# A graph-attention kernel in which ScalarE writes the exponentials twice, once to PSUM and once to SBUF

## The reference, cut to what matters

```
Qh = (h @ WQ).reshape(N, H, D);  Kh = (h @ WK).reshape(N, H, D);  Vh = (h @ WV).reshape(N, H, D)
Eh = (edge_attr @ WE).reshape(-1, H, D)
score = einsum('ehd,ehd,ehd->eh', Kh[src], Qh[dst], Eh) * inv_sqrt_d
score = exp(clip(score, -5.0, 5.0))
msg = Vh[src] * score[:, :, None]
wV = segment_sum(msg, dst, num_segments=N)
Z = segment_sum(score, dst, num_segments=N)
x = _layernorm(x + (wV / (Z[:, :, None] + 1e-06)).reshape(N, H * D))
```

## Time and profile before

| | us |
|---|---|
| median of three runs | 2854.36 |
| the three runs | 2850.20, 2854.36, 2856.99 |
| the profiled execution | 2860.5 |
| its span, first to last instruction | 2858.7 |

### The profile page before, as it was taken

The page is one execution under the profiler, slowest core; times in us unless marked ns, Lnnn a source line. Parts: engine busy times, 40 slices in busy tenths (PEclk is TensorE's granted clock), DMA queues, the critical chain, the costliest instruction groups (busy, mean ns, idle before and its releaser), DMA issues.

```text
span 2858.7 us, 39244 instructions
## 1 busy us (share of the span) xinstructions
PE 1845.5 (65%) x10440; PEld 1536.1 (54%) x10441; DVE 1490.2 (52%) x3796; ACT 1373.7 (48%) x3309; POOL 1581.0 (55%) x1629
## 2 busy tenths in 40 slices
PE   6266766767667666566666667566656676666676
PEld 5255655555555555455555555455555565555565
DVE  4154455555555555555554555555555555555567
ACT  3144554444544544454444444444444454444455
POOL 7435565555555555555555555555555565555540
PEclk9677677676777777777777777877777777777678
DMA  8335444444444444444444444444444444444431
GB/s 244 104 114 166 126 131 121 124 121 126 126 124 124 125 126 120 122 126 124 121 125 119 120 122 125 127 119 126 124 121 124 118 131 124 122 126 124 122 114 38
DMA packets 281405, 356.25 MB, mean 125 GB/s; under 512 B 144640, under 2 KB 177615, under 8 KB 281186
## 3 DMA queue, kind: packets, MB, share of 16 engines
q0 software_dynamic: 76864, 209.29, 24.9%
q1 hardware_dynamic: 203746, 144.18, 18.1%
q10 hardware_dynamic: 576, 0.26, 0.0%
HBM read 337.59 MB, written 15.97 MB: 124 GB/s over the span
## 4 chain that ended last, share of the span: by engine, by line
PE 61%; issue 33%; another core or an unknown queue 3%; DVE 1%; ACT 1%; DVEq 0%; DMA 0%; SPq 0%; ACTq 0%
PE psW L687 22%; PE psE L667 19%; PE psT L651 9%; PE psF L659 6%; PE psQ L677 4%; PE psE L610 1%; ACT hot L821 0%; PE psW L619 0%; DVE acc L1022 0%; DVE kv L901 0%; DVEq L283 0%; ACT hotT L838 0%; DMA hot<-in_x_dram 0%; ACT q_stage L793 0%
## 5 line engine op out<-in xcount | busy, mean ns | idle before, releaser
L536 POOL DMA_INDIRECT kv<-kv_table,src_idx x1580 | 1539.7, 975 | 1173.2 <-DVE msg L1077 736.8
L687 PE MATMUL psW<-msg,hot 128*128 128x136 f32 x3224 | 677.2, 373 | 891.7 <-issue 889.2
L687 PEld LDWEIGHTS psW<-msg,hot 128*128 128x128 f32 x3224 | 585.9, 264 | 935.4 <-issue 927.8
L1093 DVE TENSOR_TENSOR acc<-psW,acc 64x136 f32 x806 | 239.0, 296 | 860.6 <-remote 668.9
L667 PE MATMUL psE<-w_e,attrT 128*128 128x128 f32 x3224 | 590.6, 339 | 3.0 <-DVE prod L1056 3.0
L832 ACT ACTIVATE attrT<-psT 128x512 f32<-128x512 f32 x403 | 239.8, 595 | 727.8 <-remote 694.1
L667 PEld LDWEIGHTS psE<-w_e,attrT 128*128 128x128 f32 x3224 | 505.5, 239 | 138.8 <-issue 138.8
L821 ACT ACTIVATE hot<-iota,local 128x128 f32<-128x128 f32 x1612 | 509.0, 387 | 0.0
L1056 DVE TENSOR_TENSOR prod<-kv,psE 128x512 f32<-128x512 f32 x403 | 275.7, 684 | 363.1 <-issue 146.1
L844 ACT ACTIVATE msg<-clipped 128x32 f32<-128x32 f32 x403 | 92.3, 229 | 603.7 <-DVE clipped L1072 473.9
L651 PE MATMUL psT<-ident,attr 128*128 128x128 f32 x1612 | 348.1, 357 | 2.1 <-ACT kv L766 0.9
(11 more groups left out here) (111 smaller groups left out, 466.1 us busy)
## 6 DMA issues: line engine op xcount, KB each, us to landing
attr<-in_edge_attr_dram SPq DMA_DIRECT2D x403, 256.0 KB
kv<-kv_table,src_idx POOLq DMA_INDIRECT x1580
q_near<-q_table SPq DMA_DIRECT2D x403, 32.0 KB
kv_table<-kv SPq DMA_DIRECT2D x12, 512.0 KB
q_table<-q_stage SPq DMA_DIRECT2D x12, 384.0 KB
hot<-in_x_dram SPq DMA_DIRECT2D x12, 256.0 KB
xT<-in_x_dram SPq DMA_DIRECT2D x8, 384.0 KB
out_dram<-xT SPq DMA_DIRECT2D x45, 64.0 KB
```

The lines of the kernel that those rows point to most:

```text
L536: nc.gpsimd.indirect_dma_start(out=kv[:, g % RINGS, t, :], out_offset=None, in_=kv_table, in_offset=bass.IndirectOffsetOnAxis(ap=src_idx[: ...
L687: last = nc.tensor.matmul(psW[:, g % 2, 0:MW], hot[:, g % HOTS, t, :], msg[:, g % MSGS, t, :], start=(t == 0), stop=(t == TILES - 1))
```

## The change

ScalarE computes the exponentials of a group twice from the same clipped scores. The first instruction writes 32 columns (4 tiles x 8 heads) to `psW[g % 2]`, columns 256 to 287, and raises `exp_ok`. The second writes to `msg` in SBUF as before, and raises a new semaphore, `heads_ok`. VectorE's message product takes its second operand from PSUM. TensorE's `sum_messages` waits for `heads_ok` as well, and VectorE's clip, which overwrites the scores that both exponentials read, waits for `heads_ok` of the group before in place of `exp_ok`. The wait for a free `msg` buffer stands between the two exponentials.

```diff
+        heads_ok = sem("heads_ok")
...
+        def exp_scores(g):
+
+            return psW[:, g % 2, GROUP // 2:GROUP // 2 + TILES * HEADS].rearrange("p (t h) -> p t h", h=HEADS)
...
             def sum_messages(g):
                 pe.wait_ge(hot_ok, g + 1)
+                pe.wait_ge(heads_ok, g + 1)
                 pe.wait_ge(msg_ok, g + 1)
...
             def exponentials(g):
                 act.wait_ge(clip, g + 1)
+                scores = clipped[:, :].rearrange("p (t h) -> p t h", h=HEADS)
+                nc.scalar.activation(exp_scores(g), scores, ACT.Exp, scale=SCALE).then_inc(exp_ok, 1)
                 if g >= MSGS:
                     act.wait_ge(sums, g - MSGS + 1)
-                nc.scalar.activation(msg[:, g % MSGS, :, dim:MW], clipped[:, :].rearrange("p (t h) -> p t h", h=HEADS),
-                                     ACT.Exp, scale=SCALE).then_inc(exp_ok, 1)
+                nc.scalar.activation(msg[:, g % MSGS, :, dim:MW], scores, ACT.Exp, scale=SCALE).then_inc(heads_ok, 1)
...
                 if g >= 1:
-                    dve.wait_ge(exp_ok, g)
+                    dve.wait_ge(heads_ok, g)
...
                 nc.vector.tensor_tensor(per_head(msg[:, g % MSGS, :, 0:dim]), per_head(kv[:, g % RINGS, :, dim:2 * dim]),
-                                        msg[:, g % MSGS, :, dim:MW].unsqueeze(3).to_broadcast([P, TILES, HEADS, DH]),
+                                        exp_scores(g).unsqueeze(3).to_broadcast([P, TILES, HEADS, DH]),
```

## The result

| | before | after |
|---|---|---|
| median of four runs each, us | 2853.36 | 2944.07 |
| lowest and highest | 2850.20, 2856.99 | 2939.64, 2955.03 |
| the profiled execution (its span) | 2860.5 (2858.7) | 2955.03 (2953.3) |

The ratio is 1.0323 with a 95% interval of [1.0292, 1.0354]: 3.2% slower, 91 us, where 1.0% faster was forecast and 2872 was the top of the range.

What follows compares the result with a forecast made beforehand. A loop of GpSimd's gathers, TensorE's late results and VectorE's credit was taken as the bound. 2860.5 - 35 (gathers) + 5 (TensorE's wait) = 2830.5, or 2825 for the median, 1.0% faster; range 2802 to 2872.

Steps and rivals of the forecast that it cites:

- What bounds the kernel: No single engine: GpSimd issues gathers, TensorE's results appear after its silence, VectorE's message product then gives GpSimd new credit.
- it is seen 1.4 to 1.8 us after they stop: TensorE's work, often seen late while GpSimd issues gathers, becomes visible 1.4 to 1.8 us after the last gather ends.
- The gain: GpSimd's gathers fall from a mean of 975 to 946 ns, 46 us less issue time; three quarters count, 35 us.
- its 0.8 us is on the path: A run of twelve gathers with two long ones stands between idle times of 4.28 and 4.18 us; its 0.8 us counts.
- The rule on the ports: A VectorE operation with two SBUF inputs takes the ports shared with GpSimd, blocking its SBUF reads; one gather was 0.43 us longer.
- The product: VectorE's message product with one operand in PSUM costs +1 ns, 0 in the sum; repeated reading 28 us at most.
- The page's rule: Rival: VectorE's message product takes 0.07 us longer from PSUM, 28 us against 35 - 5, so 2852, no change; chance 0.05.
- ScalarE: One exponential more a group, 92 us more busy time, covered by ScalarE's idle time before its copy.
- TensorE's wait: One more waiting instruction before TensorE's sums costs 0 to 0.07 us a group, 28 us at most; 5 us taken.
- The first: Rival: GpSimd's gather time isn't on the path, 46 us saved becomes idle time, 2854 within 0.2%; chance 0.12.
- The rival that had the slower outcome from it: TensorE's second waiting instruction adds 0.07 us in each of 403 groups: 2882, less the gathers' gain, say 2868.
- The chance of 0.19 for slower: Slower by TensorE's wait, or by a less lucky rhythm of late releases and clock levels; the slower case reaches 2872.

Runs made afterwards that it cites:

- third comparison: Where the kernel before took 2860.97 us: changed kernel 2946.00; with a GpSimd memset of 448 columns before every fourth gather 2771.74; with 8 columns 2956.18.
- long pause: Changed kernel with two GpSimd memsets of 448 columns before every fourth gather, 0.87 us more between starts: 2706.71 us, 0.9227 of the kernel before.
- pause ahead of the first gather: Changed kernel with a GpSimd memset of 448 columns before each group's first gather: 2192.87 us, 1.0468 of the kernel before.
- four writes in a row: Changed kernel with four GpSimd memsets of 448 columns before each fourth gather: 2817.18 us, 1.3447 of the kernel before.

## Why the prediction was wrong, point by point

- **What bounds the kernel.** That no engine does, that TensorE's results are seen late and GpSimd's credit hangs on them, was right where results are held. The third comparison showed that GpSimd's issuing is a cause and not a companion of it, since a pause in it changed the time by 6%. Wrong was "it is seen 1.4 to 1.8 us after they stop" as the clock. Both numbers were in the rows, and so was the better reading: in the earlier trace rows the run from 1530.22 holds a gather of 1.38 us, and its copy still comes at 1541.78, 11.56 us after the first. The 1.8 and 1.4 differ just by the 0.4 us of the collision.
- **The gain, the step that failed.** "a gather issued faster brings the silence, the release and the next credit forward" carried 35 of the 46 us of issue time. The 46 us were saved to the digit, the collision was indeed the product's reading of SBUF beside the gather, and where results are held none of it was on the path. The earlier trace rows was read as "its 0.8 us is on the path"; its run of twelve was let on by results that passed in its middle, as its next rows show:

```profile
1435.30 0.94 POOL L536 DMA_INDIRECT kv<-kv_table,src_idx  x1 [4.28 <-DVE msg L1077]
...
1444.47 1.31 POOL L536 DMA_INDIRECT kv<-kv_table,src_idx  x1 [0.30 <-issue]
1445.35 0.60 ACT L832 ACTIVATE attrT<-psT 128x512 f32<-128x512 f32 x1 [2.67 <-remote]
```

  The copy came 10.05 us after the first gather, during the long eighth. With the delays that the collisions made the sums were seen early in 65 of 136 runs of eight, against 8 of 190 without them, and the sum had them as a cost of 35 us where their loss cost 91. Where nothing is held 39.5 us were gained and 35 had been forecast, but that is luck: there GpSimd issues nearly all the time, and the loop of silence, release and credit that the step describes isn't there.
- **The rule on the ports.** The gathers of over 1052 ns, 115 before, are gone with the second SBUF operand, and they return (means of 962 and 977 ns) where the product reads SBUF again. By the Trainium skill (SBUF — State Buffer, section "SBUF: two separate sides") that was to be so, and the trace agrees.
- **The product.** 680 ns against the 688 foreseen. The access in which each exponential is read 16 times costs nothing more from PSUM.
- **The page's rule.** The 65 ns more that the Trainium skill (VectorE: DVE Perf Modes, section "The TRN2 errata") gives an operation from PSUM don't show in 680 against 687 ns; the measurement decides against that rival.
- **ScalarE.** 201 ns for the write to PSUM and 213 for the one to SBUF, covered by idle time: 1.0008 [0.9979, 1.0037] for the second exponential alone.
- **TensorE's wait.** The bound of 0.07 us was too low, as it is 0.15, 60 us over 403 groups if all of it were on the path. It isn't: 0.9986 [0.9957, 1.0014] with the wait alone. The rival that had the slower outcome from it, by up to 28 us, was wrong in its place.
- **The rivals.** The first ("46 us less issue time become 46 us more idle time") was right in that the late results don't follow the end of the issuing, and the idle time grew, by 134.6 us and not 46; its "stays at 2854" was wrong. What was missing was a rival in which the delayed gather does something for the others, so that taking it away costs more than it frees. The chance of 0.19 for slower stood on another mechanism and too small a size; it had no way to 2944.

## What stays open

Why TensorE's results wait while gathers are issued, and where. What decides whether they do: the same kernel took 2853 to 2939 us in four places and 2096 and 2095 us in two, chip number 6 was of either kind, and no run shows what tells them apart beforehand. Whether a higher granted clock is a consequence of the prompt results (0.87 over the run against 0.74) or goes with the cause. A version in which the gathers aren't issued by GpSimd would test the picture; it wasn't tried. Nor was one with the long pause placed evenly between all gathers. The pause ahead of the first gather and the four writes in a row met only places where nothing is held, so neither where the pause should stand nor how long is too long is known. Why 30 early sums came at 8.7 to 9.2 us is open too.

## What to carry to other kernels

A stall that two engines give each other isn't a cost until it is shown to be on the path: ask what else gets through while one of them stands still, and try its removal and its replacement by a plain pause. When something is released late, measure the delay from several starting points, the first instruction of the burst among them, before the last one is called its cause; a few rounds of different length tell them apart. And a verdict on a kernel whose engines wait for something the profile can't name may turn round elsewhere (1.032 and 0.981 here), so compare in more than one place.

## What the runs showed of the hardware

- Where results are held (four of six places) TensorE's results mostly reached ScalarE only some 11.46 us (in one place 11.6) after the first of eight indirect gathers that GpSimd issued without a break, and 17.33 after the first of twelve, and VectorE 0.12 us after ScalarE or, in some runs, earlier; in the other two nothing of this is seen, and the same kernel is 27% faster (2096 against 2861 us).
- A pause of 0.34 us in every four gathers took 5.9% off the changed kernel where results are held (2946.00 to 2771.74), and one of 0.87 us 9.7% (2998.05 to 2706.71); 0.15 us did nothing (2999.33). Where nothing is held the pause of 0.34 us cost 6.6% (2058.95 to 2194.49).
- A second waiting instruction between a semaphore and TensorE's weight load took 0.15 us.
- A message product of 128x512 took 680 ns with the small operand in PSUM and 687 to 688 with it in SBUF; ScalarE wrote 128x32 exponentials in 201 ns to PSUM and 213 to 229 to SBUF.
- With both operands of the message product in SBUF 115 of 1580 gathers took 1.17 to 1.45 us, where 0.95 is usual; with one of them in PSUM none did. Where nothing is held these collisions are worth 43 us.
